# Chunked state-space mixer: per-head differences of cumulative decays moved from VectorE to ScalarE

## The reference

```python
proj = einsum('bld,pd->blp', hidden_states, in_proj_w)   # gate | x,B,C | dt
xBC  = silu(causal_conv_K4(proj[x,B,C]))
dt_p = softplus(dt + dt_bias);  A = -exp(A_log)           # 64 heads
dA   = exp(dt_p * A);  dtx = dt_p[..., None] * x
# per head h, state of 64 x 128:
state = state * dA_t + dtx_t[..., None] * B_t
y_t   = einsum('bhpn,bhn->bhp', state, C_t) + x_t * D
out   = (groupnorm(y) * norm_weight * silu(gate)) @ out_proj_w.T
```

## Time and profile before

| | |
|---|---|
| time, median of 3 runs | 3215.78 us (3214.03 to 3216.81) |
| span of the profiled execution | 3213.0 us |
| PE busy | 3077.2 us, 96% |
| DVE busy | 2594.7 us, 81% |
| ACT busy | 1327.1 us, 41% |
| POOL busy | 859.8 us, 27% |
| L706 (the differences), 1024 instructions | 378.3 us busy on DVE |

### The profile page before, as it was taken

The page is one execution under the profiler, slowest core; times in us unless marked ns, Lnnn a source line. Parts: engine busy times, 40 slices in busy tenths (PEclk is TensorE's granted clock), DMA queues, the critical chain, the costliest instruction groups (busy, mean ns, idle before and its releaser), DMA issues. The chain is left out here.

```text
span 3213.0 us, 48127 instructions
## 1 busy us (share of the span) xinstructions
PE 3077.2 (96%) x15240; PEld 2569.4 (80%) x15240; DVE 2594.7 (81%) x4252; ACT 1327.1 (41%) x2274; POOL 859.8 (27%) x899
## 2 busy tenths in 40 slices
PE   8999999999999997999999999999997999999998
PEld 6888888888888886888888887888886788887786
DVE  7888797979788887897878878797977887668777
ACT  3444343534444443453444435353533323233443
POOL 3423140504232242441322314050513000001112
PEclk9999999999999998999999999999998999999999
DMA  3322212231322213323222221213122343456564
GB/s 134 111 82 84 79 66 85 66 98 59 100 68 88 82 63 121 118 66 95 66 93 79 79 85 65 85 66 93 64 92 83 136 146 139 147 179 220 203 215 174
DMA packets 168072, 335.17 MB, mean 104 GB/s; under 512 B 14192, under 2 KB 84976, under 8 KB 167920
## 3 DMA queue, kind: packets, MB, share of 16 engines
q1 hardware_dynamic: 140880, 246.95, 24.1%
q10 hardware_dynamic: 22944, 71.84, 6.3%
q0 software_dynamic: 4096, 14.68, 1.2%
HBM read 288.85 MB, written 44.56 MB: 104 GB/s over the span
## 5 line engine op out<-in xcount | busy, mean ns | idle before, releaser
L919 PE MATMUL bank<-x_hi,w_hi 128*128 128x512 f32 x2560 | 1026.8, 401 | 0.5 <-DVE acc L680 0.5
L921 PE MATMUL bank<-x_hi,w_lo 128*128 128x512 f32 x2560 | 1000.4, 391 | 0.0
L920 PE MATMUL bank<-x_lo,w_hi 128*128 128x512 f32 x2560 | 997.6, 390 | 0.0
L680 DVE SCALAR_TENSOR_TENSOR acc<-bank,conv_w,acc 128x511 f32<-128x511 f32 (+2 forms) x576 | 431.1, 748 | 315.4 <-ACT acc L477 287.9
L921 PEld LDWEIGHTS bank<-x_hi,w_lo 128*128 128x128 f32 x2560 | 481.0, 188 | 104.3
L920 PEld LDWEIGHTS bank<-x_lo,w_hi 128*128 128x128 f32 x2560 | 482.9, 189 | 92.8
L919 PEld LDWEIGHTS bank<-x_hi,w_hi 128*128 128x128 f32 x2560 | 482.8, 189 | 92.1 <-issue 1.3
L1428 PE MATMUL bank<-wo_hi,y_hi 128*128 128x512 f32 x1024 | 401.8, 392 | 26.3 <-DVE wo_lo L1295 23.0
L1429 PE MATMUL bank<-wo_lo,y_hi 128*128 128x512 f32 x1024 | 399.9, 391 | 0.0
L1430 PE MATMUL bank<-wo_hi,y_lo 128*128 128x512 f32 x1024 | 399.7, 390 | 0.0
L477 ACT ACTIVATE acc<-bank,tap_par 128x512 f32<-128x512 f32 x192 | 149.1, 776 | 597.3 <-PE bank L921 575.3
(11 more groups left out here) (180 smaller groups left out, 4351.7 us busy)
## 6 DMA issues: line engine op xcount, KB each, us to landing
w_raw<-in_w_in SPq DMA_DIRECT2D x160, 512.0 KB, 3.6
cum_b<-cum_scratch ACTq DMA_DIRECT2D x128, 512.0 KB, 3.7
y_raw<-y_scratch SPq DMA_DIRECT2D x128, 512.0 KB, 3.3
y_scratch<-gate SPq DMA_DIRECT2D x128, 256.0 KB, 2.4
wo_raw<-in_w_out SPq DMA_DIRECT2D x128, 256.0 KB, 3.5
xbc<-in_x SPq DMA_DIRECT2D x16, 512.0 KB, 4.0
yn<-in_x SPq DMA_DIRECT2D x16, 512.0 KB, 3.6
o_sb<-in_x POOLq DMA_DIRECT2D x16, 512.0 KB, 6.5
```

The lines of the kernel that those rows point to most:

```text
L680: dve.scalar_tensor_tensor(acc[:, s % 2, back:], bank_proj[s % 2][:, 0:SEQ - back], mix.conv_w[:, g, m, 3 - back:4 - back], acc[:, s % 2, ...
L919: pe.matmul(out, w_hi[m % 2][:, k, :], hi, start=(k == 0), stop=False)
L920: pe.matmul(out, w_hi[m % 2][:, k, :], lo, start=False, stop=False)
L921: mm = pe.matmul(out, w_lo[m % 2][:, k, :], hi, start=False, stop=(k == KT - 1))
```

## The change

The eight DVE instructions of `diffs` are removed. In their place ACT computes max(cum - cum_b, 0), with the per-partition value as the bias operand of a Relu with scale -1 (`falls`), and `exps` takes the exponential with scale -1, which gives the same number. `falls` comes at the head of ACT's chunk work; in even slots `split_next_hi` now stands between `falls` and `exps`, where it stood behind `exps` before. `load_cum` and `exps` wait for the new semaphore `fall_done`.

```diff
-                need(act, diff_done, NT * g + k - 1)
+                need(act, fall_done, NT * g + k - 1)
                 act.dma_start(cum_b[:, k % 2, :, :],
...
+            def falls(g, k):
+
+                act.wait_ge(cum_loaded[k % 2], 16 * ((NT // 2) * g + k // 2 + 1))
+                need(act, multiplied, NT * g + k - 1)
+                for h in range(HPG):
+                    op = act.activation(attn[:, k % 2, h, :], cum_b[:, k % 2, h, :], ACT.Relu, scale=-1.0,
+                                        bias=mix.cum[:, chunk_tile(k), bass.ds(g * HPG + h, 1)])
+                op.then_inc(fall_done, 1)
+
             def exps(g, k):
-                act.wait_ge(diff_done, NT * g + k + 1)
-                act.activation(attn[:, k % 2, :, :], attn[:, k % 2, :, :], ACT.Exp).then_inc(exp_done, 1)
+                act.wait_ge(fall_done, NT * g + k + 1)
+                act.activation(attn[:, k % 2, :, :], attn[:, k % 2, :, :], ACT.Exp, scale=-1.0).then_inc(exp_done, 1)
...
                     if START <= s:
                         k = s - START
+                        falls(g, k)
+                        split_next_hi(g, s, last)
                         exps(g, k)
-                        split_next_hi(g, s, last)
...
-            def diffs(g, k):
-
-                dve.wait_ge(cum_loaded[k % 2], 16 * ((NT // 2) * g + k // 2 + 1))
-                need(dve, multiplied, NT * g + k - 1)
-                for h in range(HPG):
-                    op = dve.tensor_scalar(attn[:, k % 2, h, :], cum_b[:, k % 2, h, :],
-                                           mix.cum[:, chunk_tile(k), bass.ds(g * HPG + h, 1)], 0.0,
-                                           ALU.subtract, ALU.min)
-                op.then_inc(diff_done, 1)
...
-                    elif s > START:
-                        diffs(g, s - START)
...
-                            diffs(g, 0)
```

More of the change, by code:

```diff
@@ L229, in mixer_block @@
         cum_loaded = [sem("cum_loaded0"), sem("cum_loaded1")]
-        diff_done, exp_done, bc_done, dtx_done = sem("diff_done"), sem("exp_done"), sem("bc_done"), sem("dtx_done")
+        fall_done, exp_done, bc_done, dtx_done = sem("fall_done"), sem("exp_done"), sem("bc_done"), sem("dtx_done")
         dx_done, b_copied, dec_done, attn_done = sem("dx_done"), sem("b_copied"), sem("dec_done"), sem("attn_done")
```

## The result

The change made the kernel slower: 3333.56 us, median of 4 runs (3331.59 to 3338.16), against 3214.91 (3212.64 to 3216.81) before, a ratio of 1.0374 with a 95% interval of 1.0361 to 1.0387. The prediction said 3278 and at most 3322. The direction held and the size did not.

The account below looks back on a forecast made before the run. PE was taken as the bound, with its waits for dec_lo deciding the change. Span 3213.0 + 54 (chunk cycles) + 8 (clock) = 3275, plus 2.8 from span to time: 3278 us, range 3238 to 3322.

Parts of the forecast that it names:

- The bound, and the chain to dec_lo: Chunk slots: PE waits for dec_lo, 52.8 us in 57 waits, through ACT and POOL; DVE's differences are not in this chain.
- Costed at zero: Removing DVE's differences, 378.3 us of its time, was claimed to give PE nothing.
- The price of a Relu: ACT, head of chunk work: 0.29 us from start to start, 0.38 for one, 2.32 us of ACT for eight.
- POOL keeping its turn: Rival, even chunks: nvar gets in before w_lo, saving 1.1 us each, 3243 us; chance 0.14.
- cheap Relus: Two rivals: eight Relus under about 1 us, 3190 us (chance 0.07); 0.20 us each, about 3220 us (chance 0.04).
- The cycles and the clock: Chunks 0, 2, 3, 4, 5 lengthen by 3.4 us a group, 54 us in all; clock drops add 8 us.
- The waits for dec_lo: PE in chunks 2 to 5: waits near 1.9, 1.0, 2.5 and 1.1 us, about 100 us in all.
- The rival by which the clock costs its full price: Chunks 2 and 4: 32 drops cost 39 us instead of 8, 3309 us, or 3335 with dearer Relus; chance 0.13.
- my 2220: DVE's busy time after the change was claimed to be 2220 us or less.
- The convolution slots start with ACT about 2 us late, and PE has as much in its second projection tile: 0.: Convolution slots: ACT's lateness of about 2 us is covered by PE's second projection tile, costing 0.
- The 2.8 us that the forecast added from span to time: Whole kernel: the median of the runs was taken to stand 2.8 us above the span of the profile.
- My last sentence: If DVE's five instructions start earlier than 0.1 us behind the product, or convolution slots lengthen, the steps are wrong.

Follow-up runs that it names:

- run 3: Kernel before with DVE's differences kept, plus the eight Relus on ACT writing to an unused place, w_hi ahead of the exponential: 3334.38 us, ratio 1.0384.
- run 2: Kernel before with the differences left out altogether, neither DVE nor ACT computing them, ACT's order unchanged: 3199.96 us, ratio 0.9962.
- runs 1 and 6: Changed kernel with ACT's groups 2 to 6 written out instead of looped, 3290.67 us; changed kernel with hint_back_edge on ACT's loop, 3295.5 us.
- run 5: Kernel before with 128 one-column copies added to ACT's loop body, differences still on DVE: 3227.02 us, ratio 1.0046.

## Why the prediction was right and wrong

**The bound, and the chain to dec_lo: right.** PE's waits in the chunk slots are those of the chain through ACT and POOL. The differences are not in it once ACT is loaded (run 3). By themselves they are worth 12 us (run 2), which I had put at zero: chunks 2, 3 and 5 are 0.5, 0.2 and 0.2 us shorter without them. "Costed at zero" was right for the sum and not for the part taken alone.

**The price of a Relu: right.** Eight take 2.44 us, 396 ns each, where 2.41 and 0.38 were forecast. Chunk 4 of one group, with the eight Relus ahead of w_hi and exp:

```profile
1093.56 2.44 ACT L514 ACTIVATE attn<-cum_b,cum 128x128 f32<-128x128 f32 x8
...
1094.01 0.49 PE L953 MATMUL bank<-dec_hi,b_hi 128*128 128x512 f32 x1 [0.87 <-POOL dec_lo L358]
...
1095.90 1.05 ACT L461 ACTIVATE w_hi<-w_raw 128x1024 fp32r<-128x1024 f32 x1
...
1098.69 0.47 POOL L365 TENSOR_TENSOR c_lo<-xbc,c_hi 128x128 fp32r<-128x128 f32 x1 [4.74 <-ACT st_hi L546]
...
1101.35 1.17 POOL L372 TENSOR_TENSOR nvar<-ssq,eps 128x1 f32<-128x1 f32 x1
...
1103.11 1.04 POOL L351 TENSOR_TENSOR dtx_dec<-dtx,decay 128x512 f32<-128x512 f32 x1
...
1106.21 0.72 PE L953 MATMUL bank<-dec_hi,b_hi 128*128 128x512 f32 x1 [2.51 <-POOL dec_lo L358]
```

The state product of chunk 3 starts at 1094.01. c_lo starts 4.68 us behind it (forecast 1044.49 - 1039.84 = 4.65), nvar ends 8.51 behind it (8.50), PE restarts 12.20 behind it (12.23), and nvar takes 1.17 beside w_lo as the earlier trace rows had it beside L719. dtx_dec takes 1.04 instead of 1.99 (but 1.6 on average in chunk 1, where 1.05 was forecast). The rivals that rested on POOL keeping its turn, or on cheap Relus, are out.

**The cycles and the clock: right in sum.** Forecast 54 + 8 = 62 us, measured 59. Taken like the forecast from state product to state product, and with the clock in it, the means of chunks 0, 2, 3, 4 and 5 are +0.95, +1.21, +0.36, +0.88 and +0.27 us against +0.84, +0.95, +0.47, +1.02 and +0.1 without the clock. The waits for dec_lo are 1.87, 0.87 and 2.51 us in chunks 2 to 4 of this group against 1.9, 1.0 and 2.5, but chunk 3 has none in 5 groups of 16 and chunk 5 (1.1) has one in 2 only; this is why the total is 79.8 and not 100. I had every group drop the clock in chunks 2 and 4, 32 times. It fell 19 times, behind 5 of the 16 waits of chunk 2 and 14 of those of chunk 4, and where it fell (0.85 over the next cycle) PE came too late to wait in that cycle. The rival by which the clock costs its full price (54 + 39 us in the cycles) is out. DVE's busy time is 2254.5 us, over my 2220: its other instructions got longer, w_lo alone by 29 us (210.0 to 239.2).

**The step that failed: "The convolution slots start with ACT about 2 us late, and PE has as much in its second projection tile: 0."** It cost 61 us. Three things are wrong in it. The first is a size: the slack is about 0.5 us, as 2.27 us of lateness of w_hi gave 1.75 us of lateness at the second turn. What is late is w_hi, which releases w_lo on DVE, and behind that stand the convolution and `gate_y`, for which PE waits. I had looked at PE's second tile and not at DVE's queue behind w_lo. By runs 1 and 6, which have no gap at the jump, this costs 1.5 to 1.7 us a stretch; in the change it is 1.65, 23 us in 14. The second I did not have at all: the gap of about 2 us at every jump of ACT's loop, once its body had grown from 258 to 391 executed instructions. Removing it two ways saves 38 and 43 us; bringing it alone into the kernel before (run 5) makes the gap and costs 14. The third is the clock: I counted its drops in the chunk cycles only, and it falls at all eight jumps of the change as well. By run 3 that is 2.1 of the 4.8 us of a jump, 17 us of the 38. The slack that the lateness had used up is 0.5 us a jump and explains less.

**Sum.** 59 us in the chunk cycles, 23 in the stretches by ACT's lateness, 38 by the jump: 120 of 123.6 us of span. The 2.8 us that the forecast added from span to time are too many, since each execution on record shows 1.5 to 1.6 between the two. The listing that I had before the prediction shows both bodies; I read it for order and for table loads only. My last sentence named lengthening convolution slots as what would make the steps wrong, and gave it no price.

**What stays open.** ACT's body of 269 executed instructions (run 2) has no gap and one of 391 has; the lengths between were not tried, nor why DVE's loop of 435 jumps in 0.22 us. That ACT waits for a fetch is argued: from what makes the gap and what removes it, and from the packet that lies in each gap; no row names it as what released ACT. The Trainium skill (Runtime: NRT & Kernel Launch, Instruction fetch mechanics) says that such an engine holds 512 instructions and is refilled in blocks of 256, and that a "taken branch whose target isn't in the current 2-page window forces a DMA fetch of the target page before execution can continue". A gap at the backward jump, with a packet in it, agrees with that. What does not follow from it is which loops stall: the bodies of ACT and DVE are all under 512 instructions, and the longest of them, DVE's, does not. What decides whether the clock falls behind a wait of 1.5 to 4 us stays open too.

## What to carry to other kernels

An engine that is idle for half of the span can still have no room at one place of its order: put new work where the engine pauses and not at the head of its slot (3295.5 to 3209.5 us for the same Relus with the same hint). When a lot of small instructions goes into a hardware loop, count the body, waits and register instructions included, and look for a release "issue" on the first instruction of the loop; here the hint or writing the loop out removed it. Price a lateness at a stage boundary by following the late engine's product through the queues of the others to PE, not by PE's own next tile.

## What the runs showed of the hardware that I had not expected

- ACT stands 1.93 to 2.34 us at each backward jump of a body of 391 to 407 executed instructions (six kernels, 48 jumps) and not with 258 to 269, whatever the instructions do. With the hint a body of 392 has no gap. DVE's body of 435 has none either.
- TensorE's clock does not follow from the length of the wait alone: behind a wait of 3.9 us it fell at all eight jumps of the change (0.86 granted over 25 us) and stayed at 1.00 at one of run 3, and behind 1.5 us in chunk 4 it fell in 7 groups of 16 of the kernel before.
- Leaving out DVE's 1024 differences, 378.3 us of its time, made the kernel before 12 us faster, although DVE is busy for 81% of the span and PE for 96%.
